# Side operations of VectorE between a unit's scan and its product, and GpSimd's products moved to units 2, 5, 8, 10, 12, 14

## Chip, cores and metric

The kernel runs on one core of one Trainium2 chip. The metric is device time in microseconds (us), the median of the runs of one kernel.

## What is computed

Sixty-four images become 36 patch tokens each; with a class token and 77 text tokens that makes 114 tokens of width 256. One Mamba block and one feed-forward block with a mixture of experts follow, each behind a layer norm and with a residual. The core is the state-space scan over 512 channels and 16 states:

```
delta = softplus(dt @ W_dt + b_dt)
dA = exp(delta[..., None] * A)
dBu = delta[..., None] * Bm[:, :, None, :] * xc[..., None]
def step(h, inp):
    h = dA_t * h + dBu_t
    y = jnp.einsum('bdn,bn->bd', h, C_t)
```

after which y, with a skip term, is multiplied by silu(z) and projected by W_out. The shared feed-forward part is (x1 silu) times x2, a layer norm, and a projection; its rows at 512 positions are mixed with those of one of 8 experts.

## The kernel before

**Groups and units.** The batch is cut into 32 groups of two sequences (TOK = 228 tokens). The states and channels of a group are cut into 16 units, k = 0 to 15, of 128 partitions x 912 numbers. Every engine runs its own program, groups i from -2 to 32, units 0 to 15 inside; the order of the work is written out by hand, as side jobs that hang on a value of k, and a side job may belong to another group (i+2, i+1, i-1, i-2, i-3). Semaphores join the programs.

**A unit** passes through these steps. GpSimd makes dBu (`dbu`, L1646) into a ring of 8 buffers `xr`, four units ahead. ScalarE makes dA = exp(delta*A), four instructions (`exps`, L1010), into one of only two PSUM slots: unit k uses slot k % 2. VectorE scans (`scan`, L1307). Then comes the product with C (`times_c`): on VectorE (L1316), which reads the slot and writes the ring, or on GpSimd (L1654), in place in the ring, since for these units the scan writes the ring and not the slot. TensorE sums the states of the product (`reduce_states`, L711), in order of units. A slot is free for the exps of unit k+2 when the scan of k is done, if k is one of GpSimd's units, and otherwise when VectorE's product of k is done. Before, GpSimd's units are 1, 3, 8, 10, 12, 14.

**VectorE's side operations**: `ln2_stats` (L1363) and `ln2_moments` (L1372), `y_out` (L1324, y = sum times silu(z), one for units 0 to 7 and one for 8 to 15), `image_tokens` (L1329), `delta_out` (L1357), `normalize` (L1337), `ffn_gate` (L1378, then L1385 on its result), `v_norm` (L1390).

**Two chains that the prediction uses.** The window: after the exps of unit 1 ScalarE loads a table, computes silu for x of group i+1 (`x_silu`) and for z of group i (`z_silu`, L1047), whose second half waits for a projection by TensorE (`proj_z`, L610) that itself waits for x_silu; then it loads the other table and makes the exps of unit 2. The softplus chain: `v_norm` (VectorE) - `ffn_out` (TensorE, L782, L783) - `out_copy` (ScalarE, L1122) - `proj_delta` (TensorE, L697) - softplus in three instructions (ScalarE, L1058, L1062, L1066) - `delta_out` (VectorE, behind unit 7's scan) - `u_out` (GpSimd, L1667), the factor of the next group's dBu, which passes through DRAM, as delta does.

Of the kernel before, what the change touches and what calls it, by code (L numbers as in the profile page):

```python
# [12 lines left out]
EPS = 1e-5  # L13
BIG = 1e30
A_TOP = -1e-26
ON_POOL = (1, 3, 8, 10, 12, 14)


def fusion_kernel(nc, x_patches, txt_t, tok_w, tok_b, cls_t, pos_t, w_in, conv_w, conv_b, w_x, w_dt, b_dt,
# [28 lines left out]
    MT = M // P  # L48
    E = gate_w.shape[2] - 1

    ON_DVE = tuple(k for k in range(UNITS) if k not in ON_POOL)
    N_DVE, N_POOL = len(ON_DVE), len(ON_POOL)

    bc_scratch = nc.dram_tensor("bc_scratch", (2, 2 * NS, TOK), F32, kind="Internal").ap()
    u_scratch = nc.dram_tensor("u_scratch", (2, 2, J, DQ, 2 * TOK), F32, kind="Internal").ap()
# [6 lines left out]
    with ExitStack() as whole:  # L62
# [20 lines left out]
        with ExitStack() as ctx:  # L83
# [329 lines left out]
            def need(e, semaphore, value):  # L413

                if not isinstance(value, int) or value > 0:
                    e.wait_ge(semaphore, value)
# [18 lines left out]

            def product_done(e, i, k):

                if k in ON_POOL:
                    e.wait_ge(c_pool, N_POOL * i + ON_POOL.index(k) + 1)
                else:  # L440
                    e.wait_ge(c_dve, N_DVE * i + ON_DVE.index(k) + 1)

            with nc.Block() as block:

# [160 lines left out]
                def _(pe):  # L605
# [140 lines left out]
                    def ffn_in(g):  # L746
                        pe.wait_ge(x2t_ev, g + 1)

                        if g < GROUPS - 2:
                            pe.wait_ge(h2_ev, g + 2)  # L750
                        else:
                            pe.wait_ge(scan_done, UNITS * GROUPS)
                            pe.wait_ge(c_dve, N_DVE * GROUPS)
                        for a in range(2):
                            for k in range(DC):
                                mm = pe.matmul(f12_ps(g)[:, a], w12[:, k, a * H:(a + 1) * H], x2t[:, k].rearrange("p s t -> p (s t)"),  # L756
                                               start=(k == 0), stop=(k == DC - 1))
                        mm.then_inc(f12_mm, 1)
# [160 lines left out]
                    def hidden(m, j):  # L919
                        if m >= 1:  # L920
                            pe.wait_ge(a_done, 2 * m - 1 + j)
                        elif j == 0:

                            pe.wait_ge(scan_done, UNITS * GROUPS)
                            pe.wait_ge(c_dve, N_DVE * GROUPS)
                        else:
                            pe.wait_ge(o_done, GROUPS)
                        for half in range(2):
                            for k in range(DC):
                                mm = pe.matmul(psum[:, 2 * j + half, :], xmt[:, k, m],  # L930
                                               (e1, e2)[j][:, k, half * 512:(half + 1) * 512],
                                               start=(k == 0), stop=(k == DC - 1))
                        mm.then_inc(h12_mm, 1)
# [60 lines left out]
                def _(act):  # L994
                    def exps(i, p, k):

                        c, n, v = k // NI, k % NI, UNITS * i + k
                        if k == 0:
                            act.wait_ge(delta_in[0], 16 * NQ * (i + 1))
                        if k == UNITS // 2:  # L1000
                            act.wait_ge(delta_in[1], 16 * NQ * (i + 1))

                        back = (k - SLOTS) % UNITS
                        step = i if k >= SLOTS else i - 1
                        if back in ON_POOL:
                            need(act, scan_done, v - SLOTS + 1)
                        else:
                            need(act, c_dve, N_DVE * step + ON_DVE.index(back) + 1)
                        for j in range(J):
                            ins = nc.scalar.activation(slot(k)[:, j * TOK:(j + 1) * TOK], delta4[:, c // 2, j, c % 2], ACT.Exp,  # L1010
                                                       scale=a_neg[:, c, j, n:n + 1])
                        ins.then_inc(exp_done, 1)
# [287 lines left out]
                def _(dve):  # L1300
                    def scan(i, k):

                        v = UNITS * i + k
                        dve.wait_ge(exp_done, v + 1)
                        dve.wait_ge(dbu_done, v + 1)
                        x = xr[:, k % XRING].rearrange("p j t -> p (j t)")
                        nc.vector.tensor_tensor_scan(x if k in ON_POOL else slot(k), slot(k), x, 0.0,  # L1307
                                                     ALU.mult, ALU.add).then_inc(scan_done, 1)

                    def times_c(i, p, k):  # L1310
                        if k in ON_POOL:
                            return
                        if k == ON_DVE[0]:
                            dve.wait_ge(c_in, 16 * NQ * (i + 1))
                        dve.wait_ge(scan_done, UNITS * i + k + 1)
                        nc.vector.tensor_tensor(xr[:, k % XRING], slot(k).rearrange("p (j t) -> p j t", j=J),  # L1316
                                                cbc[:, p, k % NI].unsqueeze(1).to_broadcast([P, J, TOK]),
                                                ALU.mult).then_inc(c_dve, 1)
# [54 lines left out]
                        ins.then_inc(mv2_done, 1)  # L1373

                    def ffn_gate(g):

                        dve.wait_ge(fs_done, g + 1)
                        nc.vector.scalar_tensor_tensor(out=gate_of(g), in0=f12_ps(g)[:, 0], scalar=b1[:, 0:1], in1=gate_of(g),  # L1378
                                                       op0=ALU.add, op1=ALU.mult).then_inc(gate_done, 1)
                        dve.wait_ge(gate_done, g + 1)  # L1380
                        if g < GROUPS - 2:
                            need(dve, f3_mm, g)
                        else:
                            ffn_free(dve, g)
                        nc.vector.scalar_tensor_tensor(out=vv_of(g), in0=f12_ps(g)[:, 1], scalar=b2[:, 0:1], in1=gate_of(g),  # L1385
                                                       op0=ALU.add, op1=ALU.mult).then_inc(v_done, 1)
# [23 lines left out]
                    def body(i):  # L1410
                        p = i % 2
                        q = 1 - p
                        if i == -1:
                            return before_first()
                        if i == GROUPS:
                            return after_last()
                        for k in range(UNITS):
                            if k == 1 and runs(i - 2):
                                ln2_ready(i - 2)
                            if runs(i):  # L1420
                                scan(i, k)
                            if k == 3 and runs(i + 2):
                                image_tokens(i + 2)
                            if k == 1 and runs(i - 1):
                                y_out(i - 1, q, 1)
                            if k == 9 and runs(i + 2):
                                normalize(i + 2, p)
                            if k == 7 and runs(i + 1):
                                delta_out(i + 1)
                            if runs(i):  # L1430
                                times_c(i, p, k)
                            if k == 0 and runs(i - 2):
                                ln2_moments(i - 2)
                            if k == 15 and runs(i - 2):
                                ffn_gate(i - 2)
                            if k == 4 and runs(i - 3):
                                v_norm(i - 3)
                            if k == 15 and runs(i - 1):
                                ln2_stats(i - 1)
                            if k == 10 and runs(i):  # L1440
                                y_out(i, p, 0)

                    count = [0]

# [188 lines left out]
                def _(pool):  # L1633
# [14 lines left out]
                                                ALU.mult).then_inc(dbu_done, 1)  # L1648

                    def times_c(i, p, k):  # L1650
                        if k == ON_POOL[0]:
                            pool.wait_ge(c_in, 16 * NQ * (i + 1))
                        pool.wait_ge(scan_done, UNITS * i + k + 1)
                        nc.gpsimd.tensor_tensor(xr[:, k % XRING], xr[:, k % XRING],  # L1654
                                                cbc[:, p, k % NI].unsqueeze(1).to_broadcast([P, J, TOK]),
                                                ALU.mult).then_inc(c_pool, 1)
# [22 lines left out]
                    def body(i):  # L1679
# [2 lines left out]
                        if i == 6:  # L1682
                            expert_constants()
                        for k in range(UNITS):
                            if runs(i) and k in ON_POOL:
                                times_c(i, p, k)
                            if k + LEAD < UNITS:
                                if runs(i):
# [119 lines left out]
```

## Time and profile before

| | |
|---|---|
| time, median of 3 runs | 1729.16 us (1728.2 to 1730.28) |
| profiled execution, from the first to the last instruction (its own time as far as the profile has one) | 1726.7 us |
| VectorE busy | 1555.7 us (90%) |
| GpSimd busy | 1564.6 us (91%) |
| TensorE busy | 1480.7 us (86%) |
| ScalarE busy | 1331.9 us (77%) |

The profile is of one execution. Its span is 2.5 us under the median of the timed runs; what lies around the span is taken as constant. Rows of a timeline give start, duration, engine, line, operation, written and read tiles, count, and in brackets the idle time before it with what ended it. An instruction's start may lie a little before the end of the one ahead of it, so costs are read as distances from start to start.

### The profile page before, as it was taken

The numbers are of one execution on the slowest core, as the hardware profiler recorded it, in microseconds if no ns is written. First come the engines' busy times: TensorE is split into PE (matmuls) and PEld (weight loads), VectorE is DVE, ScalarE is ACT, GpSimd is POOL, SyncE is SP. The second block draws the span as 40 slices with busy tenths as digits, with TensorE's granted clock in tenths as the row PEclk, the third lists the DMA queues.
The fourth block names the chain that finished last, engine by engine and source line by source line (L and its number), as shares of the span: only waits on it lengthen the run. The fifth ranks groups of instructions, "written<-read, shape, count | busy, mean of one in ns | idle before, by whom it ended". The sixth has DMA issues, their size and how long they took to land.

```text
span 1726.7 us, 28038 instructions
## 1 busy us (share of the span) xinstructions
PE 1480.7 (86%) x9868; PEld 1065.4 (62%) x9868; DVE 1555.7 (90%) x1389; ACT 1331.9 (77%) x3100; POOL 1564.6 (91%) x782
## 2 busy tenths in 40 slices
PE   7778898889888988898889889888889898977688
PEld 7555666666666666666666666666666666654355
DVE  2599999999999999999999999999999999999944
ACT  2577788888888888888888888888888888886644
POOL 0699999999999999999999999999999999999814
PEclk9888999999999999999999999999999999997899
DMA  4667755555656655656666555566665555656110
GB/s 141 138 135 180 163 130 123 122 131 132 145 129 146 132 123 122 131 130 146 129 146 135 122 125 126 130 146 129 145 138 121 125 126 129 142 119 141 36 34 15
DMA packets 194430, 218.47 MB, mean 127 GB/s; under 512 B 94011, under 2 KB 184773, under 8 KB 193778
## 3 DMA queue, kind: packets, MB, share of 16 engines
q1 hardware_dynamic: 193522, 215.51, 56.6%
q8 instruction: 78, 1.28, 0.3%
q0 software_dynamic: 576, 1.17, 0.3%
q14 instruction: 62, 0.51, 0.1%
q10 hardware_dynamic: 192, 0.01, 0.0%
HBM read 169.92 MB, written 47.09 MB: 126 GB/s over the span
## 4 chain that ended last, share of the span: by engine, by line
DVE 41%; ACT 18%; issue 16%; PE 13%; POOL 10%; DMA 2%; SPq 0%; DVEq 0%; ACTq 0%; POOLq 0%
DVE psum L1307 20%; DVE xr L1307 16%; ACT psum L1010 6%; POOL xr L1646 6%; POOL xr L1654 3%; PE psum L610 3%; DVE xr L1316 3%; ACT L1132 2%; PE psum L697 2%; PE psum L782 2%; ACT L1041 2%; ACT soft L1062 2%; ACT soft L1066 2%; ACT soft L1058 2%; PE psum L783 1%
## 5 line engine op out<-in xcount | busy, mean ns | idle before, releaser
L1646 POOL TENSOR_TENSOR xr<-u,bbc 128x912 f32<-128x912 f32 x512 | 1075.5, 2133 | 14.3 <-DMA u<-u_scratch 13.9
L1010 ACT ACTIVATE psum<-delta,a_neg 128x228 f32<-128x228 f32 x2048 | 805.9, 441 | 221.6 <-DVE xr L1316 191.2
L1307 DVE TENSOR_TENSOR_SCAN psum<-psum,xr 128x912 f32<-128x912 f32 x320 | 656.2, 2051 | 68.5 <-ACT psum L1010 59.8
L1654 POOL TENSOR_TENSOR xr<-xr,cbc 128x912 f32<-128x912 f32 x192 | 409.2, 2131 | 31.9 <-DVE xr L1307 28.5
L1307 DVE TENSOR_TENSOR_SCAN xr<-psum,xr 128x912 f32<-128x912 f32 x192 | 392.3, 2043 | 0.0
L1316 DVE TENSOR_TENSOR xr<-psum,cbc 128x912 f32<-128x912 f32 x320 | 353.7, 1105 | 11.1
L711 PE MATMUL psum<-xr,fold 128*32 128x228 f32 x4096 | 295.1, 385 | 50.6 <-POOL xr L1654 26.7
L610 PE MATMUL psum<-xh,win 128*128 128x228 f32 x1024 | 222.7, 367 | 61.8 <-ACT xs L1041 33.4
L610 PEld LDWEIGHTS psum<-xh,win 128*128 128x128 f32 x1024 | 192.1, 193 | 91.7 <-ACT xs L1041 44.0
L661 PE MATMUL psum<-xi,conv_d 128*128 128x228 f32 x1024 | 210.9, 358 | 0.0
L711 PEld LDWEIGHTS psum<-xr,fold 128*32 128x32 f32 x4096 | 96.9, 112 | 178.1 <-issue 79.4
L661 PEld LDWEIGHTS psum<-xi,conv_d 128*128 128x128 f32 x1024 | 190.2, 188 | 16.2 <-issue 11.7
L730 PE MATMUL psum<-wout,y 128*114 128x256 f32 x512 | 134.8, 411 | 0.0
L708 PE MATMUL psum<-xs,skip_w 128*128 128x228 f32 x256 | 83.2, 408 | 30.0 <-DVE y L1324 30.0
L730 PEld LDWEIGHTS psum<-wout,y 128*114 128x114 f32 x512 | 97.4, 200 | 18.8
L625 PE MATMUL psum<-xp,tokw 128*128 128x72 f32 x768 | 92.3, 278 | 8.4 <-DMA xp<-x_patches 8.4
L625 PEld LDWEIGHTS psum<-xp,tokw 128*128 128x128 f32 x768 | 92.8, 196 | 10.0 <-DMA xp<-x_patches 8.9
L1667 POOL TENSOR_TENSOR u<-delta,xs 128x912 f32<-128x912 f32 x31 | 65.9, 2125 | 18.4 <-issue 12.0
L708 PEld LDWEIGHTS psum<-xs,skip_w 128*128 128x128 f32 x256 | 40.9, 194 | 67.1 <-DVE y L1324 44.4
L697 PE MATMUL psum<-dbl,wdt 17*128 17x228 f32 x256 | 58.7, 369 | 22.2 <-ACT ob L1122 21.8
L697 PEld LDWEIGHTS psum<-dbl,wdt 17*128 17x128 f32 x256 | 46.0, 189 | 36.6 <-issue 34.0
L756 PE MATMUL psum<-x2t,w 128*128 128x228 f32 x256 | 58.8, 374 | 1.9
(204 smaller groups left out, 1574.7 us busy)
## 6 DMA issues: line engine op xcount, KB each, us to landing
delta<-delta_scratch SPq DMA_DIRECT2D x256, 228.0 KB, 6.5
u<-u_scratch SPq DMA_DIRECT2D x256, 228.0 KB, 4.2
bbc<-bc_scratch SPq DMA_DIRECT2D x128, 114.0 KB, 2.6
u_scratch<-u SPq DMA_DIRECT2D x64, 228.0 KB, 4.9
cbc<-bc_scratch SPq DMA_DIRECT2D x128, 114.0 KB, 2.7
delta_scratch<-delta SPq DMA_DIRECT2D x64, 226.0 KB, 5.7
out<-ob SPq DMA_DIRECT2D x32, 228.0 KB
h_scratch<-h SPq DMA_DIRECT2D x31, 228.0 KB
```

Of the source, the lines that this page charges most:

```text
L610: mm = pe.matmul(bank[:, c], win[:, k, at + c * P:at + (c + 1) * P], xh[:, p, k], start=(k == 0), stop=(k == DC - 1))
L625: mm = pe.matmul(tok_ps[:, c, g % 2:g % 2 + count].rearrange("p h t -> p (h t)"), tokw[:, k, c * P:(c + 1) * P], xp[:, k, g % 2:g % 2 + co ...
L661: mm = pe.matmul(conv_bank(half)[:, c].rearrange("p (s t) -> p s t", s=SEQ), conv_d[:, at, t], xi[:, at, :, t:t + T], start=(t == 0), stop ...
L697: mm = pe.matmul(dt_bank(half)[:, c], wdt[32:33 + R, (2 * half + c) * P:(2 * half + c + 1) * P], dbl[32:33 + R, :], start=True, stop=True)
L708: pe.matmul(y_ps, skip_w[:, c], xs[:, i % 2, c], start=True, stop=False)
L711: mm = pe.matmul(y_ps[j * DQ:(j + 1) * DQ], fold[:], xr[:, k % XRING, j], start=False, stop=(n == NI - 1))
L730: mm = pe.matmul(h2_ps[:, s], y[:, g % 2, c, s * T:(s + 1) * T], wout[:, c], start=False, stop=(c == CH - 1))
L1010: ins = nc.scalar.activation(slot(k)[:, j * TOK:(j + 1) * TOK], delta4[:, c // 2, j, c % 2], ACT.Exp, scale=a_neg[:, c, j, n:n + 1])
L1307: nc.vector.tensor_tensor_scan(x if k in ON_POOL else slot(k), slot(k), x, 0.0, ALU.mult, ALU.add).then_inc(scan_done, 1)
L1316: nc.vector.tensor_tensor(xr[:, k % XRING], slot(k).rearrange("p (j t) -> p j t", j=J), cbc[:, p, k % NI].unsqueeze(1).to_broadcast([P, J, ...
L1646: nc.gpsimd.tensor_tensor(xr[:, k % XRING], u4[:, c // 2, :, c % 2], bbc[:, p, n].unsqueeze(1).to_broadcast([P, J, TOK]), ALU.mult).then_i ...
L1654: nc.gpsimd.tensor_tensor(xr[:, k % XRING], xr[:, k % XRING], cbc[:, p, k % NI].unsqueeze(1).to_broadcast([P, J, TOK]), ALU.mult).then_inc ...
```

## The change

GpSimd's products are those of units 2, 5, 8, 10, 12, 14 in place of 1, 3, 8, 10, 12, 14: VectorE has those of 1 and 3 and gives up 2 and 5; each engine has as many as before. VectorE's program has a new order in each group. `ln2_ready` and `ln2_moments`, which stood around unit 0's product, stand between scan and product of unit 0; `y_out` of the group before stays behind scan 1, which now has a product after it; the first half of `ffn_gate` goes in front of product 15, the second half stays behind it; `y_out` of the group's own first half moves from behind scan 10 to between scan and product of unit 11. `image_tokens` (3), `delta_out` (7) and `normalize` (9) keep their places between scan and product. The other engines keep their programs but for the place of GpSimd's two products and the values waited for.

```diff
-ON_POOL = (1, 3, 8, 10, 12, 14)
+ON_POOL = ((2, 5, 8, 10, 12, 14),)
...
-                        if back in ON_POOL:
+                        if step < 0 or back in on_pool(step):
                             need(act, scan_done, v - SLOTS + 1)
                         else:
-                            need(act, c_dve, N_DVE * step + ON_DVE.index(back) + 1)
+                            act.wait_ge(c_dve, dve_products(step, back) + 1)
...
                     def ffn_gate(g):
+                        ffn_first(g)
+                        ffn_second(g)
...
                         for k in range(UNITS):
-                            if k == 1 and runs(i - 2):
-                                ln2_ready(i - 2)
                             if runs(i):
                                 scan(i, k)
+                            if k == 0 and runs(i - 2):
+                                ln2_ready(i - 2)
+                            if k == 0 and runs(i - 2):
+                                ln2_moments(i - 2)
+                            if k == 1 and runs(i - 1):
+                                y_out(i - 1, q, 1)
                             if k == 3 and runs(i + 2):
                                 image_tokens(i + 2)
-                            if k == 1 and runs(i - 1):
-                                y_out(i - 1, q, 1)
+                            if k == 7 and runs(i + 1):
+                                delta_out(i + 1)
                             if k == 9 and runs(i + 2):
                                 normalize(i + 2, p)
-                            if k == 7 and runs(i + 1):
-                                delta_out(i + 1)
+                            if k == 11 and runs(i):
+                                y_out(i, p, 0)
+                            if k == 15 and runs(i - 2):
+                                ffn_first(i - 2)
                             if runs(i):
                                 times_c(i, p, k)
-                            if k == 0 and runs(i - 2):
-                                ln2_moments(i - 2)
-                            if k == 15 and runs(i - 2):
-                                ffn_gate(i - 2)
                             if k == 4 and runs(i - 3):
                                 v_norm(i - 3)
+                            if k == 15 and runs(i - 2):
+                                ffn_second(i - 2)
                             if k == 15 and runs(i - 1):
                                 ln2_stats(i - 1)
-                            if k == 10 and runs(i):
-                                y_out(i, p, 0)
```

## Rows read from the trace of the kernel before

**Rows 1.** Page, part 1: busy time, share and instructions of each engine.
```profile
PE 1480.7 (86%) x9868; PEld 1065.4 (62%) x9868; DVE 1555.7 (90%) x1389; ACT 1331.9 (77%) x3100; POOL 1564.6 (91%) x782
```

**Rows 2.** Timeline of VectorE (DVE): the sums that close two groups.
```profile
208.60 0.74 DVE L1363 BATCH_NORM_STATS2 st<-h 114x6 f32<-114x256 f32 x2
...
1538.69 0.74 DVE L1363 BATCH_NORM_STATS2 st<-h 114x6 f32<-114x256 f32 x2
```

**Rows 3.** Timeline of VectorE, one group from unit 15 of the one before.
```profile
847.13 1.11 DVE L1316 TENSOR_TENSOR xr<-psum,cbc 128x912 f32<-128x912 f32 x1
848.16 0.45 DVE L1378 SCALAR_TENSOR_TENSOR gate<-psum,b,gate 128x228 f32<-128x228 f32 x1
848.64 0.46 DVE L1385 SCALAR_TENSOR_TENSOR vv<-psum,b,gate 128x228 f32<-128x228 f32 x1
849.01 0.74 DVE L1363 BATCH_NORM_STATS2 st<-h 114x6 f32<-114x256 f32 x2
849.67 2.05 DVE L1307 TENSOR_TENSOR_SCAN psum<-psum,xr 128x912 f32<-128x912 f32 x1
851.82 1.11 DVE L1316 TENSOR_TENSOR xr<-psum,cbc 128x912 f32<-128x912 f32 x1
...
854.95 0.60 DVE L1324 TENSOR_TENSOR y<-psum,sz 128x456 f32<-128x456 f32 x1
857.33 2.06 DVE L1307 TENSOR_TENSOR_SCAN psum<-psum,xr 128x912 f32<-128x912 f32 x1 [1.78 <-ACT psum L1010]
859.43 1.11 DVE L1316 TENSOR_TENSOR xr<-psum,cbc 128x912 f32<-128x912 f32 x1
860.46 2.05 DVE L1307 TENSOR_TENSOR_SCAN xr<-psum,xr 128x912 f32<-128x912 f32 x1
...
865.73 0.38 DVE L1390 TENSOR_TENSOR vv<-vv,psum 128x228 f32<-128x228 f32 x1
...
872.26 2.05 DVE L1307 TENSOR_TENSOR_SCAN psum<-psum,xr 128x912 f32<-128x912 f32 x1
874.22 1.09 DVE L1357 SCALAR_TENSOR_TENSOR delta<-psum,soft 128x912 f32<-128x912 f32 x1
...
896.40 1.11 DVE L1316 TENSOR_TENSOR xr<-psum,cbc 128x912 f32<-128x912 f32 x1
```

**Rows 4.** Timeline of ScalarE (ACT) in that group.
```profile
853.86 0.55 ACT L1047 ACTIVATE sz<-psum 128x456 f32<-128x456 f32 x1 [0.77 <-PE psum L610]
...
855.72 1.58 ACT L1010 ACTIVATE psum<-delta,a_neg 128x228 f32<-128x228 f32 x4
...
865.95 1.57 ACT L1010 ACTIVATE psum<-delta,a_neg 128x228 f32<-128x228 f32 x4
868.19 0.60 ACT L1122 ACTIVATE ob<-psum 114x512 f32<-114x512 f32 x1 [0.67 <-PE psum L783]
...
872.75 0.96 ACT L1066 ACTIVATE soft<-soft 128x912 f32<-128x912 f32 x1
```

**Rows 5.** Timeline of TensorE (PE) in that group.
```profile
853.75 0.98 PE L711 MATMUL psum<-xr,fold 128*32 128x228 f32 x16
...
866.17 0.69 PE L782 MATMUL psum<-h,plus 115*114 115x256 f32 x2 [0.61 <-DVE vv L1390]
```

**Rows 6.** Timeline of GpSimd (POOL) in that group.
```profile
864.67 10.44 POOL L1646 TENSOR_TENSOR xr<-u,bbc 128x912 f32<-128x912 f32 x5
875.45 2.12 POOL L1667 TENSOR_TENSOR u<-delta,xs 128x912 f32<-128x912 f32 x1 [0.34 <-issue]
878.37 2.12 POOL L1654 TENSOR_TENSOR xr<-xr,cbc 128x912 f32<-128x912 f32 x1 [0.80 <-DVE xr L1307]
```

**Rows 7.** Busy time by stretch; the granted clock is the third figure from the end.
```profile
857.33:874.22 16.89, 15.50 (x104) 10.41 (x103) 16.75 (x12) 15.25 (x36) 16.78 (x9) 0.91 0.30 85
...
869.00:871.00 2.00, 2.00 (x10) 1.60 (x10) 2.00 (x2) 1.74 (x5) 2.00 (x2) 1.00 0.40 110
871.00:873.00 2.00, 2.00 (x19) 0.61 (x17) 1.97 (x3) 1.94 (x3) 2.00 (x2) 0.52 0.14 49
873.00:875.00 2.00, 2.00 (x16) 1.32 (x12) 2.00 (x2) 2.00 (x5) 2.00 (x2) 0.63 0.00 0
```

**Rows 8.** Timeline of VectorE in the last group but one: idle before delta.
```profile
1566.65 1.11 DVE L1357 SCALAR_TENSOR_TENSOR delta<-psum,soft 128x912 f32<-128x912 f32 x1 [2.87 <-issue]
```

**Rows 9.** Busy time by stretch, that group.
```profile
1538.70:1590.30 51.60, 34.36 (x216) 20.65 (x216) 46.53 (x37) 38.07 (x90) 47.51 (x24) 0.81 0.53 119
```

More of the change, by code:

```diff
@@ L49, in fusion_kernel, with on_pool, pool_products, dve_products @@
     E = gate_w.shape[2] - 1
-    ON_DVE = tuple(k for k in range(UNITS) if k not in ON_POOL)
-    N_DVE, N_POOL = len(ON_DVE), len(ON_POOL)
+    def on_pool(g):
+        return ON_POOL[g % len(ON_POOL)]
+    def pool_products(g, k):
+        return sum(len(on_pool(a)) for a in range(g)) + sum(x < k for x in on_pool(g))
+    def dve_products(g, k):
+        return UNITS * g + k - pool_products(g, k)
+    ALL_DVE = dve_products(GROUPS, 0)
     bc_scratch = nc.dram_tensor("bc_scratch", (2, 2 * NS, TOK), F32, kind="Internal").ap()
@@ L436, in product_done @@
             def product_done(e, i, k):
-                if k in ON_POOL:
-                    e.wait_ge(c_pool, N_POOL * i + ON_POOL.index(k) + 1)
+                if k in on_pool(i):
+                    e.wait_ge(c_pool, pool_products(i, k) + 1)
                 else:
-                    e.wait_ge(c_dve, N_DVE * i + ON_DVE.index(k) + 1)
+                    e.wait_ge(c_dve, dve_products(i, k) + 1)
             with nc.Block() as block:
@@ L752, in ffn_in @@
                             pe.wait_ge(scan_done, UNITS * GROUPS)
-                            pe.wait_ge(c_dve, N_DVE * GROUPS)
+                            pe.wait_ge(c_dve, ALL_DVE)
                         for a in range(2):
@@ L924, in hidden @@
                             pe.wait_ge(scan_done, UNITS * GROUPS)
-                            pe.wait_ge(c_dve, N_DVE * GROUPS)
+                            pe.wait_ge(c_dve, ALL_DVE)
                         else:
@@ L1306, in scan @@
                         x = xr[:, k % XRING].rearrange("p j t -> p (j t)")
-                        nc.vector.tensor_tensor_scan(x if k in ON_POOL else slot(k), slot(k), x, 0.0,
+                        nc.vector.tensor_tensor_scan(x if k in on_pool(i) else slot(k), slot(k), x, 0.0,
                                                      ALU.mult, ALU.add).then_inc(scan_done, 1)
                     def times_c(i, p, k):
-                        if k in ON_POOL:
+                        if k in on_pool(i):
                             return
-                        if k == ON_DVE[0]:
+                        if dve_products(i, k) == dve_products(i, 0):
                             dve.wait_ge(c_in, 16 * NQ * (i + 1))
@@ L1375, in ffn_gate, with ffn_first @@
                     def ffn_gate(g):
+                        ffn_first(g)
+                        ffn_second(g)
+                    def ffn_first(g):
                         dve.wait_ge(fs_done, g + 1)
@@ L1379, in ffn_gate, with ffn_second @@
                                                        op0=ALU.add, op1=ALU.mult).then_inc(gate_done, 1)
+                    def ffn_second(g):
                         dve.wait_ge(gate_done, g + 1)
@@ L1650, in times_c @@
                     def times_c(i, p, k):
-                        if k == ON_POOL[0]:
+                        if k == on_pool(i)[0]:
                             pool.wait_ge(c_in, 16 * NQ * (i + 1))
@@ L1684, in body @@
                         for k in range(UNITS):
-                            if runs(i) and k in ON_POOL:
+                            if runs(i) and k in on_pool(i):
                                 times_c(i, p, k)
```

## The prediction

> **What bounds the kernel now.** I read the page first: by share of busy time VectorE (90%) and GpSimd (91%) are level [rows 1], which says only that neither leaves much room. The timeline of VectorE says more. From group 3 to 29 every group takes the same time: the closing statistics stand at 208.60 and 1538.69 us, 27 groups apart [rows 2], so 49.26 us a group. Inside a group I cut VectorE's row of work at three points [rows 3]: A from the end of product 15 (847.13 + 1.11 = 848.24) to the scan of unit 2 (857.33), 9.09 us; B from there to delta (874.22), 16.89 us; C from delta to the end of the next product 15 (896.40 + 1.11 = 897.51), 23.29 us. Sum 49.27. The reader is to see that B and C have no idle time and that A has 1.78 us of it, ended by ScalarE: this is the window, whose exps of unit 2 run from 855.72 for 1.58 us [rows 4] and end just before that scan. The window starts when product 15 is done, so A is a length that ScalarE and TensorE set (z_silu waits 0.77 us for TensorE in it), and not VectorE's work.
>
> GpSimd issues its 22 products per group 2.09 us apart (five in 10.44 us) and u_out takes 2.12: 48.0 us. The rest of its group is waiting: 0.34 us for delta and 0.80 us for scan 8 [rows 6]. So no change of VectorE alone can bring a group under 48.0.
>
> **What a filled pair is worth.** A scan and the product that waits for it stand 2.10 us apart (857.33 to 859.43), 2.15 at unit 0 (849.67 to 851.82), whereas scan 7 and delta, which doesn't wait for that scan, stand 1.96 apart (872.26 to 874.22). The same shows in small: gate to vv, dependent, 0.48 us for an instruction of 0.45; vv to statistics, independent, 0.37 for one of 0.46 [rows 3]. So an operation put between two dependent ones hides 0.13 us and costs only its own distance. The Trainium skill ("VectorE: DVE Perf Modes", section "The DRAIN you can't avoid") says the contrary: a semaphore between chained operations costs nothing extra, the flush comes anyway. These rows disagree with it; what it would make of the time is the second rival.
>
> Dependent pairs of scan and product: before, units 0, 2, 4, 5, 6, 11, 13, 15, eight (7 and 9 are filled already); after, 4, 6, 13, three. The dependent pair in ffn_gate goes too.
>
> **A after the change.** ffn_first (0.48) leaves it, unit 0's pair is filled (0.19), product 1 comes in (1.03). VectorE's own work was 9.09 - 1.78 = 7.31, and is now 7.67: still under 9.09, so product 1 costs nothing, the window covers it. Were that cover gone it would cost 1.03. The window itself is not moved: it still starts with product 15's end, and none of its instructions changes. y_out of the group before would start 6.1 us after product 15's end; TensorE's last two reductions end at 853.75 + 0.98 = 854.73 [rows 5], 6.5 after it, because they are queued behind the projection that waits for x_silu. So y_out waits some 0.5 us, then product 1 ends about 8.3 after, still inside 9.09. Behind y_out only product 1 is queued. A stays 9.09.
>
> **B after the change.** Products 2 and 5 leave, product 3 comes: -1.03. Pairs 2 and 5 are no longer dependent pairs, 3 is a filled one: -0.26. VectorE would reach delta at 16.89 - 1.29 = 15.60. What is late next is the softplus chain. Before, v_norm ended at 865.73 + 0.38 = 866.11, TensorE waited for it (0.61 us, L782), ScalarE waited for TensorE (0.67, L1122), and the last softplus instruction ended at 872.75 + 0.96 = 873.71 [rows 3 to 5], 7.60 after v_norm and 16.38 after scan 2: a slack of 0.5 to delta. v_norm is hardly moved (product 2 before it goes, product 3 comes, one pair saved: 0.13 earlier), so softplus ends at 16.2. VectorE waits 0.6 us and B becomes 16.22, not 15.60. Nothing on VectorE but product 7 stands behind delta at that point; GpSimd's u_out is no longer held by it, see below.
>
> Exps have a tighter due time here: unit 6's wait for product 4, which ends at 8.34 after scan 2; ScalarE comes to them at 865.95, that is 8.62, as before, and they end at 10.19, 0.3 before scan 6 (10.51). Unit 3's exps end about 0.05 before scan 3, now that no product stands in front of it; a delay there falls into the 0.6 us of waiting before delta.
>
> **C after the change.** Pairs 11 and 15 are filled: -0.26. ffn_first comes in front of product 15: +0.37. y_out moves inside C, one instruction, no change. C = 23.40. Product 15 is later by that 0.37, and the window hangs on it; this is paid here. On TensorE, y_out's move by 1.3 us holds the reduction of unit 8, and with it the convolution that x_silu waits for: worked through the queue, it ends 0.6 us after product 15, and x_silu comes at 2.9 after it. No cost; 2.3 us of cover.
>
> **GpSimd.** Product 2 can start only at scan 2's end, 2.1 after scan 2. From unit 8's product its row reaches unit 2's 14 products later, 29.2 us, where the scan is done at about 30.4. So it waits there, runs some 1.3 us later than before in the rest of the group, and has 0.7 us of slack in all. dBu for unit 12 comes 4 us before its scan. u_out ends 0.9 us later after scan 2, and the exps of unit 0 come 0.9 earlier; their delta, through DRAM, lands about 1 us late for them at worst, but they are not due before the exps of unit 1, 1.5 us later. No cost, little cover.
>
> **The sum.** 9.09 + 16.22 + 23.40 = 48.71 against 49.27: 0.56 us a group, 15.1 us over 27 groups. Groups 1 and 31 have no softplus wait of this kind and get about 1.1 each, group 2 0.5, group 0 some 0.2, the last but one nothing, since its delta waits for softplus already [rows 8]; the late product 15 of the last group costs 0.4. Together 17.6; for the early clock fall that the last rival speaks of I take 0.6 off: 17. From the span, 1726.7 - 17 = 1709.7; with the 2.5 us around it, 1712.
>
> **Rivals.**
> First, softplus does not hold delta, because TensorE comes through its part sooner. Then VectorE runs at 9.09 + 15.60 + 23.40 = 48.09, just above GpSimd's 48.0: 1.18 a group, 32 + 2 us, 1695. For it: TensorE waits for v_norm and not the reverse, and has idle time. Against: each link of the chain shows as a wait in the rows. Chance 0.12.
>
> Second, a filled pair saves nothing. Then A is 9.09, B is held by softplus at 16.41, C is 23.29 + 0.37 = 23.66: 49.16, a gain of 0.1 a group, 1726. The skill's rule of the page named above gives this; the rows speak against it. Chance 0.05.
>
> Third, the saving is real and part of it is lost again in C, to exps that come late with one scan between them and the product they wait for (11, 13, 15: 0.25 us of room at most), or to product 1's lateness, or the DRAM round of delta. 0.2 to 0.5 us a group: 1718 to 1728. Chance 0.17.
>
> Fourth, on the other side: TensorE's clock. Its mean is 0.91 in B, between the two levels (1.2 and 2.4 GHz): in this group it is full until 871 us, and 0.52 and 0.63 in the two stretches behind it [rows 7]. That is 14 us after scan 2, just behind the chain's TensorE part, and most groups have one such fall. In the last group but one, where TensorE had less work (34.36 us busy) and mean clock 0.81 [rows 9], delta waited 2.87 us [rows 8]. With softplus now on the path, a fall some microseconds earlier costs 2.87 + 0.5, about 3.4 us, in each group where it happens; five such groups of 27 eat the gain, more make the kernel slower: ten give 1712 + 34 = 1746. For it: y_out's move opens a new idle stretch of about 1.4 us on TensorE. Against: that stretch is 14 us behind the chain, and TensorE's work per group is unchanged in a shorter group. Chance 0.13.
>
> **Numbers.** The forecast has 0.53, with 1706 to 1717 as its own range. With the first rival's nearer half and the third, 1698 to 1726 leaves out some 0.2. No change from before is what lies within 0.2%, 3.5 us, about what a measurement of this kernel tells: 1725.7 to 1732.6. Faster 0.78 (forecast, first, most of the third), same 0.09 (second, the rest of the third), slower 0.13 (fourth).
>
> **What the profile after would show.** Right: scans of 0, 1, 3, 7, 9, 11, 15 stand 1.96 ahead of the next instruction; the idle time before scan 2 falls to about 0.9 with 0.5 before y_out; delta has a new idle time near 0.6; GpSimd waits at product 2 and not at 8; a group takes 48.7. No idle time before delta and 48.1 a group means the first rival; 2.1 between a scan and a filler the second; idle time before scans of 11, 13 or 15 the third; a lower granted clock in the 13 us behind scan 2, and 2 to 3 us before delta, the fourth. The prediction is wrong above all if a wait that I did not price comes into B or C, since nothing there absorbs it.

## The result, and the profile after

The changed kernel takes 1710.57 us (median of 4 runs, 1709.33 to 1713.89), against 1728.84 us for the kernel before in the same session. The ratio is 0.9895, with a 95% interval of 0.9881 to 0.9909: 1.05% faster. The prediction was 1712. The profiled execution has a span of 1708.0 us, 18.7 less than before. In the experiments one execution of e6, of 2433.86 us at a mean granted clock of 0.544, is left out of the comparisons.

Part 1 of the page after (busy time and share of each engine), to be held against [rows 1]: VectorE does the same work in 11 us less of busy time, and the shares hardly move.

```profile
PE 1483.6 (87%) x9868; PEld 1065.3 (62%) x9868; DVE 1544.3 (90%) x1389; ACT 1328.5 (78%) x3100; POOL 1563.2 (92%) x782
```

The page says no more than that. The timeline of VectorE for one group does, the counterpart of [rows 3]:

```profile
840.29 1.10 DVE L1326 TENSOR_TENSOR xr<-psum,cbc 128x912 f32<-128x912 f32 x1
841.30 0.44 DVE L1401 SCALAR_TENSOR_TENSOR vv<-psum,b,gate 128x228 f32<-128x228 f32 x1
841.67 0.74 DVE L1373 BATCH_NORM_STATS2 st<-h 114x6 f32<-114x256 f32 x2
...
847.94 0.63 DVE L1334 TENSOR_TENSOR y<-psum,sz 128x456 f32<-128x456 f32 x1 [0.39 <-PE psum L721]
848.49 1.10 DVE L1326 TENSOR_TENSOR xr<-psum,cbc 128x912 f32<-128x912 f32 x1
850.48 2.06 DVE L1317 TENSOR_TENSOR_SCAN xr<-psum,xr 128x912 f32<-128x912 f32 x1 [0.89 <-ACT psum L1020]
...
857.71 1.11 DVE L1326 TENSOR_TENSOR xr<-psum,cbc 128x912 f32<-128x912 f32 x1
858.73 0.38 DVE L1406 TENSOR_TENSOR vv<-vv,psum 128x228 f32<-128x228 f32 x1
...
864.09 2.05 DVE L1317 TENSOR_TENSOR_SCAN psum<-psum,xr 128x912 f32<-128x912 f32 x1
866.81 1.11 DVE L1367 SCALAR_TENSOR_TENSOR delta<-psum,soft 128x912 f32<-128x912 f32 x1 [0.67 <-issue]
...
878.22 0.61 DVE L1334 TENSOR_TENSOR y<-psum,sz 128x456 f32<-128x456 f32 x1
878.75 1.09 DVE L1326 TENSOR_TENSOR xr<-psum,cbc 128x912 f32<-128x912 f32 x1
...
888.73 0.43 DVE L1392 SCALAR_TENSOR_TENSOR gate<-psum,b,gate 128x228 f32<-128x228 f32 x1
889.08 1.10 DVE L1326 TENSOR_TENSOR xr<-psum,cbc 128x912 f32<-128x912 f32 x1
890.46 0.74 DVE L1373 BATCH_NORM_STATS2 st<-h 114x6 f32<-114x256 f32 x2
```

Cut at the same three points: A from 840.29 + 1.10 = 841.39 to 850.48, 9.09 us, with 0.39 us of idle time before y_out and 0.89 before scan 2; B to 866.81, 16.33, with 0.67 before delta; C to 889.08 + 1.10 = 890.18, 23.37, with none. Sum 48.79; the statistics stand 890.46 - 841.67 = 48.79 apart as well. Over the groups from 450 to 1500 us the median of each part is the same within 0.01.

The links of the softplus chain, in the timelines of TensorE and ScalarE of that group (counterparts in [rows 4, 5]):

```profile
859.17 0.69 PE L792 MATMUL psum<-h,plus 115*114 115x256 f32 x2 [0.59 <-DVE vv L1406]
...
861.93 1.77 PE L707 MATMUL psum<-dbl,wdt 17*128 17x228 f32 x8 [0.78 <-ACT ob L1132]
```
```profile
861.19 0.60 ACT L1132 ACTIVATE ob<-psum 114x512 f32<-114x512 f32 x1 [0.64 <-PE psum L793]
...
863.79 0.93 ACT L1068 ACTIVATE soft<-psum 128x912 f32<-128x912 f32 x1 [0.54 <-issue]
...
865.75 0.97 ACT L1076 ACTIVATE soft<-soft 128x912 f32<-128x912 f32 x1
```

v_norm ends at 858.73 + 0.38 = 859.11, the last softplus instruction at 866.72, 7.61 later; scan 7 was over at 866.14, and delta starts at 866.81, 0.09 after softplus. Its row names no releaser ("issue"), so that it waits for softplus is read from these times; e3 tests it. The idle time of GpSimd has moved from product 8 [rows 6] to product 2:

```profile
852.68 2.13 POOL L1672 TENSOR_TENSOR xr<-xr,cbc 128x912 f32<-128x912 f32 x1 [0.70 <-DVE xr L1317]
```

### The profile page after: what moved, and what is told of

Same layout as the page of the kernel before. It is cut to its first block, busy times and chain, and to the rows that moved or that the text cites. A ratio compares the mean times of both kernels' runs of the same rounds, so it can differ in the third digit from the quotient of the medians.

```text
span 1708.0 us, 28038 instructions
## 1 busy us (share of the span) xinstructions
PE 1483.6 (87%) x9868; PEld 1065.3 (62%) x9868; DVE 1544.3 (90%) x1389; ACT 1328.5 (78%) x3100; POOL 1563.2 (92%) x782
## 4 chain that ended last, share of the span: by engine, by line
DVE 24%; POOL 19%; ACT 18%; issue 13%; PE 12%; DMA 12%; SPq 2%; DVEq 0%; ACTq 0%; POOLq 0%
DVE psum L1317 12%; POOL xr L1664 12%; ACT psum L1020 7%; DMA u<-u_scratch 7%; DVE xr L1317 5%; DVE xr L1326 5%; PE psum L620 4%; DMA u_scratch<-u 4%; POOL u L1685 3%; ACT L1142 2%; POOL xr L1672 2%; ACT L1051 2%; PE psum L792 2%; SPq L482 2%; ACT soft L1068 2%
## 5 line engine op out<-in xcount | busy, mean ns | idle before, releaser
L740 PEld LDWEIGHTS psum<-wout,y 128*114 128x114 f32 x512 | 96.7, 198 | 18.7
L792 PE MATMUL psum<-h,plus 115*114 115x256 f32 x124 | 41.6, 418 | 24.0 <-DVE vv L1406 24.0
```

What stands on the lines that cost most here:

```text
L740: mm = pe.matmul(h2_ps[:, s], y[:, g % 2, c, s * T:(s + 1) * T], wout[:, c], start=False, stop=(c == CH - 1))
```

## The experiments

A, B, C and the period are medians over the groups from 450 to 1500 us of each profiled execution. Each time is a median of its own runs, and the ratio is against the kernel before on the same chip, which took 1728.2 to 1730.35 us on the four chips used. The changed kernel itself was timed in its own session only, so distances between variants of 2 us or less say nothing. All variants start from the changed kernel. In e3, e6 and e11 product 7 stands in front of delta and so counts in B, not in C.

| kernel | time, us | ratio (95%) | A | B | C | group |
|---|---|---|---|---|---|---|
| before | 1728.84 | | 9.09 | 16.89 | 23.28 | 49.26 |
| changed | 1710.57 | 0.9895 (0.9881 to 0.9909) | 9.09 | 16.34 | 23.36 | 48.79 |
| e1, only the units | 1710.51 | 0.9902 (0.9887 to 0.9917) | 9.09 | 16.33 | 23.30 | 48.72 |
| e2, only the order | 1728.64 | 1.0003 (0.9994 to 1.0012) | 9.09 | 16.89 | 23.34 | 49.32 |
| e3, delta behind product 7 | 1693.56 | 0.9792 (0.9778 to 0.9805) | 9.09 | 16.73 | 22.34 | 48.16 |
| e4, gate behind product 15 | 1705.52 | 0.9868 (0.9852 to 0.9883) | 9.09 | 16.33 | 23.16 | 48.58 |
| e5, y_out behind scan 10 | 1715.88 | 0.9919 (0.9905 to 0.9932) | 9.09 | 16.34 | 23.51 | 48.94 |
| e7, extra in A | 1709.16 | 0.9877 (0.9861 to 0.9893) | 9.09 | 16.34 | 23.36 | 48.79 |
| e8, extra in C | 1730.63 | 1.0009 (0.9997 to 1.0021) | 9.09 | 16.34 | 24.02 | 49.45 |
| e9, GpSimd 1, 5 | 1761.38 | 1.0170 (1.0150 to 1.0189) | 9.09 | 17.50 | 23.36 | 49.95 |
| e10, GpSimd 2, 3 | 1722.12 | 0.9957 (0.9942 to 0.9972) | 9.09 | 16.71 | 23.36 | 49.16 |
| e6, both moves (profile at a clock of 0.902) | 1687.83 | 0.9757 (0.9744 to 0.9770) | 9.14 | 16.73 | 22.25 | 48.12 |
| e11, e6 once more | 1688.31 | 0.9787 (0.9756 to 0.9819) | 9.09 | 16.73 | 22.14 | 47.95 |

**Which half of the change carries the gain.** Two runs, each with one half. e1 puts VectorE's old order of the side operations back; e2 the old units of GpSimd:

```diff
-ON_POOL = ((2, 5, 8, 10, 12, 14),)
+ON_POOL = ((1, 3, 8, 10, 12, 14),)
```

> The changed kernel with VectorE's order of before: only GpSimd's units are new. Theory (the move of the products carries the gain; A, window, stays 9.09 us, B is held by softplus at 16.3, C gets 0.26 for two unfilled pairs and loses the 0.37 of the gate's first half in front of product 15): 48.68 us a group against 48.79, so some 3 us under the changed kernel, 1707 to 1708. Rival (the filled pairs carry the gain): six pairs of 0.11 to 0.13 come back on the path, 49.4 us a group, 1729 or more.

> The changed kernel with GpSimd's units of before (1, 3, 8, 10, 12, 14): only VectorE's order is new. Theory: A 9.09 (held by the window, what is saved there is idle time), B 16.89 as before the change (pairs 2, 4, 5, 6 are unfilled in both), C 23.40: 49.38 us a group, 0.11 more than before the change, 1732 us. Rival (the filled pairs carry the gain): 0.5 us a group under before, 1712 to 1715.

Measured: e1 takes what the changed kernel takes, e2 what the kernel before takes; its B is 16.89 again. So the units carry the gain, as the first theory has it, and the rivals with the filled pairs fall. Both times missed what was expected by 3 us. e1 was to be 3 us under the changed kernel; its group is 0.07 us shorter (0.11 expected), 2 us in 28 groups, and the time shows none of it. e2 came out at 1728.64 and not 1732. Its median group takes 49.32 us (49.38 expected), and in seven of 22 groups A is 9.39. In its trace 26 steady groups take 3.6 us more than before (1284.4 against 1280.8), but what follows VectorE's last product takes 4.3 us less (84.3 against 88.6). That last part is 84.1 to 86.1 us in every profile but two, that of the kernel before and that of e6 (90.5); there is one trace of the kernel before, and why it is longer there isn't shown.

**Is delta really held by softplus, and what is next.** e3 lets product 7 run while softplus is late:

```diff
-                            if k == 7 and runs(i + 1):
-                                delta_out(i + 1)
...
                             if runs(i):
                                 times_c(i, p, k)
+                            if k == 7 and runs(i + 1):
+                                delta_out(i + 1)
```

> The changed kernel with delta behind product 7 instead of in front of it: the product runs while softplus is late, at the price of one unfilled pair (0.13). Theory (softplus holds delta, nothing else is near): scan 8 stands 17.75 us behind scan 2 instead of 18.37, no idle time before delta, 48.17 us a group, 28 x 0.62 = 17 us faster than the changed kernel, 1693. Rival (GpSimd with its 48.0 us and its wait at product 2, or the trip of u and delta through DRAM, is as near): less than half of it, 1702 or more, with new waits of GpSimd or of the exps of units 0 and 1 for a DMA.

Measured 1693.56 us and 48.16 us a group. In the timeline of VectorE of e3 no idle time is left before delta:

```profile
889.14 2.06 DVE L1317 TENSOR_TENSOR_SCAN xr<-psum,xr 128x912 f32<-128x912 f32 x1 [0.89 <-ACT psum L1020]
...
904.84 1.11 DVE L1326 TENSOR_TENSOR xr<-psum,cbc 128x912 f32<-128x912 f32 x1
905.87 1.10 DVE L1367 SCALAR_TENSOR_TENSOR delta<-psum,soft 128x912 f32<-128x912 f32 x1
906.88 2.06 DVE L1317 TENSOR_TENSOR_SCAN xr<-psum,xr 128x912 f32<-128x912 f32 x1
```

Scan 8 stands 906.88 - 889.14 = 17.74 us behind scan 2 (17.75 expected), against 18.37 in the changed kernel (868.85 - 850.48). One instruction moved down by one place gives another 17 us, nearly as much as the change itself.

**The gate in front of or behind product 15.** My sum had ffn_first in front of product 15 as a loss, since the window hangs on that product. e4 puts it back behind:

```diff
-                            if k == 15 and runs(i - 2):
-                                ffn_first(i - 2)
                             if runs(i):
                                 times_c(i, p, k)
+                            if k == 15 and runs(i - 2):
+                                ffn_first(i - 2)
```

> The changed kernel with both halves of the gate behind product 15, as before the change. Theory (the window starts at product 15's end and covers what follows it): C falls by 0.37 and gets back the 0.13 of the unfilled pair, A stays 9.09, 48.55 us a group, 0.24 x 28 = 7 us faster than the changed kernel, 1704. Rival (a dependent pair costs wherever it stands, and the length of A is VectorE's): pair 15 and the gate's pair come back, 0.24 us a group slower, 1717.

Measured 1705.52, 5 us under the changed kernel (7 expected); C loses 0.20 and A stays 9.09, in which the gate's two halves now lie. A filled pair in C was thus bought with 0.35 us on the path to save 0.13. What stands in A costs the kernel nothing.

**What one filled pair is worth.** e5 takes y_out of the first half back behind scan 10:

```diff
-                            if k == 11 and runs(i):
-                                y_out(i, p, 0)
...
+                            if k == 10 and runs(i):
+                                y_out(i, p, 0)
```

> The changed kernel with y_out of the first half behind scan 10 again; pair 11 is unfilled. Theory (an unfilled pair costs 0.11 to 0.13 us where VectorE is the bound): scan 11 and product 11 stand 2.09 apart, C 23.49 instead of 23.36, 48.92 us a group, 1714. Rival (a filled pair saves nothing, as a rule says): C and the time stay, 1710.5.

Measured 1715.88 us, and C is longer by 0.15. The rows of e5 around unit 11:

```profile
877.94 0.61 DVE L1334 TENSOR_TENSOR y<-psum,sz 128x456 f32<-128x456 f32 x1
878.47 2.06 DVE L1317 TENSOR_TENSOR_SCAN psum<-psum,xr 128x912 f32<-128x912 f32 x1
880.56 1.11 DVE L1326 TENSOR_TENSOR xr<-psum,cbc 128x912 f32<-128x912 f32 x1
881.58 2.04 DVE L1317 TENSOR_TENSOR_SCAN xr<-psum,xr 128x912 f32<-128x912 f32 x1
```

y_out costs 0.53 in both places; scan to product is 2.09 here and 1.95 from scan to y_out in the changed kernel (876.27 to 878.22). The product waits for a semaphore of the scan in front of it, and y_out for none. The Trainium skill's sentence in "VectorE: DVE Perf Modes", section "The DRAIN you can't avoid", that a semaphore between chained operations costs nothing extra, was measured there on eight copies and does not hold for this pair. The same section also says that a next operation that is not held starts earlier, and the 1.95 us agree with that. A filled pair is worth 0.13 us where VectorE is the bound and nothing in A or ahead of a late delta.

**Where VectorE's work is free.** e7 and e8 add one instruction to each group, a maximum over 576 columns of a constant tile into a column that nobody reads; in e7 behind product 1, in e8 behind scan 12:

```diff
+            spare = sb("spare", [P, 1])
...
+                            if k == 1 and runs(i):
+                                nc.vector.tensor_reduce(spare[:], tokw[:].rearrange("p k d -> p (k d)")[:, 0:576], AX.X, ALU.max)
```

> The changed kernel with one more instruction on VectorE behind product 1, inside A: a maximum over 576 columns of a constant tile, some 0.6 us (estimate from y_out, 0.52 for 456 columns), its result unused. Theory (A is the window of ScalarE and TensorE, VectorE idles 0.89 in it): idle time before scan 2 falls to 0.3, a group stays 48.79, 1710.5. Rival (A is VectorE's work): +0.6 a group, 1729.

> The changed kernel with the same extra instruction behind scan 12, inside C, its result unused. Theory (nothing in C absorbs VectorE's work): +0.6 a group, 49.4, 1710.5 + 31 x 0.6 = 1729. Rival (GpSimd or the trip through DRAM is the real bound of a group and VectorE only follows): less than half of it, under 1720.

Measured 1709.16 and 1730.63 us. In e7 the instruction eats idle time:

```profile
848.76 0.74 DVE L1456 TENSOR_REDUCE spare<-tokw 128x1 f32<-128x576 f32 x1
849.74 2.06 DVE L1318 TENSOR_TENSOR_SCAN xr<-psum,xr 128x912 f32<-128x912 f32 x1 [0.23 <-ACT psum L1021]
```

in e8 the same instruction adds 0.66 us to C and 20 us to the kernel, more than the change gained. So VectorE's work is free in A and paid in full in C; no other experiment shows this so plainly.

**Each of the two moved products alone.** I expected this to split the gain cleanly:

```diff
-ON_POOL = ((2, 5, 8, 10, 12, 14),)
+ON_POOL = ((1, 5, 8, 10, 12, 14),)
```

(e9; e10 has 2, 3, 8, 10, 12, 14.)

> The changed kernel with GpSimd's units 1, 5, 8, 10, 12, 14: of the two moves of products only that of 3 to 5 is made; product 2 is VectorE's and product 1 isn't. Theory (the gain comes from the product that goes into the idle time of A): A 9.09, B 16.76 (product 3 in, 5 out, one unfilled pair less than before the change), C 23.36: 49.21 us a group, 1726. Rival (each of the two moved products gives half): 49.05, 1719.

> The changed kernel with GpSimd's units 2, 3, 8, 10, 12, 14: only the move of 1 to 2 is made; product 1 is VectorE's, in A, and product 2 leaves B. Theory: A 9.09, VectorE would reach delta after 15.73, softplus holds it at 16.33 all the same, C 23.36: 48.78 us a group, as the changed kernel, 1710.5. Rival (each of the two moved products gives half): 49.05, 1719.

Both missed, by 35 and 12 us, and each in the softplus chain, which I had priced in the prediction and took as given here. VectorE's rows of one group of e9:

```profile
827.37 2.06 DVE L1317 TENSOR_TENSOR_SCAN psum<-psum,xr 128x912 f32<-128x912 f32 x1 [1.90 <-ACT psum L1020]
...
836.79 0.38 DVE L1406 TENSOR_TENSOR vv<-vv,psum 128x228 f32<-128x228 f32 x1
...
846.27 1.11 DVE L1367 SCALAR_TENSOR_TENSOR delta<-psum,soft 128x912 f32<-128x912 f32 x1 [1.46 <-ACT soft L1076]
```

v_norm stands behind the products 2, 3 and 4 and starts 9.42 us after scan 2, not 8.25. With 0.38 and the 7.6 of the chain softplus would be ready at 17.4, and in the median group B is 17.50, 0.74 above the 16.76 expected: 21 of the 35 us. The rest is in other groups: the mean period is 50.7, the median 49.95. In nine of the 21 groups between 450 and 1500 us B is 18.9 to 20.2, as it is here (18.90), and in these the clock falls inside the chain. TensorE's rows and the clock of the same group:

```profile
837.22 0.84 PE L792 MATMUL psum<-h,plus 115*114 115x256 f32 x2 [1.75 <-DVE vv L1406]
837.85 1.06 PE L793 MATMUL psum<-w,vv 128*114 128x256 f32 x2
838.71 1.06 PE L792 MATMUL psum<-h,plus 115*114 115x256 f32 x2
839.56 1.06 PE L793 MATMUL psum<-w,vv 128*114 128x256 f32 x2
```
```profile
836.00:838.00 2.00, 0.78 (x3) 0.63 (x4) 2.00 (x3) 2.00 (x6) 1.16 (x1) 0.91 0.84 230
838.00:840.00 2.00, 2.00 (x7) 1.41 (x5) 2.00 (x2) 0.50 (x2) 0.79 (x1) 0.50 0.34 108
```

The granted clock, third from the end, is 0.50 from 838 to 840, the lower of the two levels; the matmuls take 1.06 us instead of 0.60 and delta waited 1.46 us. In the other twelve groups TensorE waits the same 1.75 us for v_norm and the matmuls behind it take 0.60, so that wait alone doesn't decide whether the clock falls; what does isn't shown.

In e10, products 2 and 3 are both GpSimd's. Its rows of one group:

```profile
856.25 2.13 POOL L1672 TENSOR_TENSOR xr<-xr,cbc 128x912 f32<-128x912 f32 x1 [1.25 <-DVE xr L1317]
858.34 2.12 POOL L1664 TENSOR_TENSOR xr<-u,bbc 128x912 f32<-128x912 f32 x1
860.41 2.13 POOL L1672 TENSOR_TENSOR xr<-xr,cbc 128x912 f32<-128x912 f32 x1
```

Product 3 is done at 862.54, 8.5 us after scan 2 (854.05); TensorE's queue has reduction 3 in front of ffn_out and waits for it (19.3 us in 20 waits between 400 and 1400 us), a place in a queue that the prediction had not looked at, and delta is held till 16.71. The moves are not halves of the gain. The move of 1 to 2 alone gains 8 us on the kernel before (0.9957), the move of 3 to 5 alone loses 31 (1.0170), and on top of the first it gains: it takes product 3 back from GpSimd, and the two together gain 18.

**Both paying moves together.** e6 has the edits of e3 and e4; e11 is the same kernel.

> The changed kernel with both moves that paid alone: delta behind product 7 (48.16 us a group) and the gate behind product 15 (0.22 less). Theory: VectorE alone would come to 47.94 us a group, GpSimd's 22 products and u_out take 48.0; so GpSimd is the bound, it waits for nobody, 48.0 to 48.1 us a group, and the second move gives 0.1 to 0.15 instead of 0.22: 1689 to 1690. Rival (GpSimd has more room than its rows show, or the gains add): 47.94 or less, 1687. Third (the trip of delta through DRAM delays the exps of units 0 and 1, so the window starts late): 48.2 or more, A longer than 9.09, no gain over the delta move alone.

> The kernel with both moves once more, since its profiled execution took 10 us more than its median and had TensorE's clock at 0.90. If GpSimd's 22 products and u_out are the floor, the rows of a group without disturbance show GpSimd with no wait at all and 48.0 to 48.1 us a group, and the time is 1689 or more; if the gains just add, a group takes 47.94 or less, with waits left on GpSimd, and the time is 1687.

Measured 1687.83 us and 1688.31. The profiled execution of e6 took 1697.69, ten more than its median, and one of e11's four took 1697.12, both at a mean granted clock of 0.90; no other kernel here shows this, and its cause is open. The profiled execution of e11 is near its median, and there a group takes 47.95. By its time and its period this is the case in which the gains add, which I had not expected; but GpSimd has no wait between 400 and 1400 us, which was to be the sign of the other case. GpSimd's product of unit 2 in two groups, one behind the other, in e11:

```profile
841.52 2.16 POOL L1672 TENSOR_TENSOR xr<-xr,cbc 128x912 f32<-128x912 f32 x1
...
889.49 2.14 POOL L1672 TENSOR_TENSOR xr<-xr,cbc 128x912 f32<-128x912 f32 x1
```

Between these two rows it has no idle time with a releaser, and they stand 47.97 us apart, the 48.0 of the prediction. VectorE idles 0.89 in A, as before. So in e11 the cycle of the window and VectorE (47.96 in this group) and GpSimd's own work (47.97) are level, and which of them holds the period can't be told. This version is 2.1 to 2.4% faster than the kernel before (by the two ratios; the interval of e11, 0.9756 to 0.9819, reaches from 1.8 to 2.4%) and 1.3% faster than the changed one.

## Why the prediction was right, step by step

- **A stays 9.09, product 1 is free.** Right: the median is 9.09 in all profiles but that of e6. Idle time before y_out was put at 0.5 and is 0.39; before scan 2 it was put at 0.9 and is 0.89. e7 shows the cover, e1 that the new order is not needed for it.
- **B is not 15.60 but 16.22, held by softplus.** Right, and 0.11 short: 16.33. The chain took 7.61 us, as read from before: v_norm started 8.25 us after scan 2, 0.15 earlier than before (0.13 forecast), ended at 8.63, and the softplus instructions ended at 16.24. Delta then started 0.09 after that, which the sum had left out; the 16.22 is also 0.03 less than its own terms give (16.38 - 0.13). e3 shows that the wait is for softplus.
- **C is 23.40.** Measured 23.36: ffn_first costs 0.35 instead of 0.37. e4 and e5 show both its terms.
- **GpSimd.** The wait moved to product 2 as said, 0.70 us. Its distance of 48.0 us was right to 0.03 (e11).
- **The sum.** 0.56 us a group was forecast over 27 groups, 15.1 us; 0.47 was measured, 12.7 us. The other groups and the ends gave 6.0 where I had taken 2.9 - 0.4 - 0.6 = 1.9. The span is 1.7 us below the 1709.7 worked out. So two errors of opposite sign nearly cancel, and that the time comes so near 1712 is in part luck: 4.5 us of the 18.7 lie behind VectorE's last product (84.1 us against 88.6), a part that the prediction did not price. e2, with the old units, has 84.3 us there, so it isn't the product moves that shorten it.
- **First rival** (softplus doesn't hold): it did. e3 takes the wait off VectorE by another way, at the price of one unfilled pair, and its 1693.56 is near the 1695 given for a kernel without the wait.
- **Second rival** (a filled pair saves nothing): fell, by e5. But its kin holds: of the three pairs that only the new order fills (1 and 3 are filled in the old one too), 0 lies in A and brings nothing, 11 brings 0.13, and 15 costs more than it brings. As a whole the order costs 0.06 to 0.07 us a group and nothing that the timed runs tell (e1, e2).
- **Third rival** (exps late in C): no idle time appeared in C.
- **Fourth rival** (the clock): the mean over the span is nearly as before, 0.949 against 0.947. In the group whose statistics stand at 402.57 us, delta waited 1.23 us with a clock of 0.61 from 374 to 378 us, and that group took 0.56 us more; in no other of the steady groups is B longer by more than 0.2 us. In e9, where TensorE waits longer for v_norm, it comes in nine of 21 groups and costs 1.4 to 2.7 us each, less than the 3.4 of the prediction. So the mechanism is real, and its price was put too high. What keeps it off the changed kernel isn't shown; e9 goes with a longer idle time of TensorE in front of the chain, but most of its groups have that idle time without the fall.

What the prediction lacked is the other side of its own sum: it had A's window fixed and ffn_first at 0.37 in front of it, and did not say that the order's part of the change was a small loss that the units carried.

## What to carry to other kernels

Cut the steady period of the busiest engine at the points where something else holds it, and price each edit by the piece it falls into: the same instruction of 0.66 us was free in one piece and cost 20 us in another. When an engine's work is shortened in front of a join, work out the other branch of the join from the rows at once; it tells how much of the gain arrives, and often the next move, which here was to let the instruction that waits change places with one that doesn't. A product moved to a slower engine moves also in every queue that takes results in order, so what one move is worth can depend on another: that of 3 to 5 cost 31 us alone and gained 10 on top of that of 1 to 2.

## What was not expected of the hardware

A dependent pair on VectorE costs 0.13 us more than an independent one for 912 columns (2.09 against 1.96) and 0.11 to 0.13 for 228 columns, nearly the same: the first half of the gate stands 0.48 in front of the second half, which needs it, and 0.35 in front of product 15, which doesn't; the second half stands 0.37 in front of the statistics. TensorE's clock fell inside the chain in nine of 21 groups of e9, behind a wait of 1.75 us for v_norm that all of its groups have, and the matmuls there took 1.06 us instead of 0.60; with a wait of 0.59 us at the same place in the changed kernel the clock was full through B in the group shown:

```profile
850.48:866.81 16.33, 14.84 (x111) 9.79 (x110) 15.60 (x11) 14.71 (x35) 15.53 (x8) 1.00 0.32 88
```
